# A transformer block on one core: output weights centred on the chip, second norm and residual addition as one VectorE instruction per chunk

## The reference

```python
x = x + LN(attn(LN(x)))     # l1 norm inside, l2 norm outside
x = x + LN(ffn(LN(x)))      # l3 norm inside, z norm outside

def attn(x):
    q = silu(x @ Wq1 @ Wq2)
    f = sigmoid(x @ Wk1 @ Wk2); a = exp(log_sigmoid(f)); k = 1 - a
    h = scan over the tokens of  a * h + k * (x @ Wv)
    out = q * h
    out = out * rsqrt(mean(out * out) + 1e-6) * norm_w      # 512 features
    return out @ Wo                                         # to 256 features

def ffn(x):                 # 6 blocks, a layer norm with gain and bias between them
    x = gelu(x @ W1.T + b1) @ W2.T + b2 + x                 # 256 -> 1024 -> 256
```

## Time and profile before

| | us |
|---|---|
| median of 3 runs (663.36 to 664.93) | 663.96 |
| the profiled execution's own time | 664.71 |
| its span, first to last instruction | 662.9 |
| PE busy | 641.2 (97%) |
| DVE busy | 450.7 (68%) |
| ACT busy | 411.6 (62%) |
| POOL busy | 282.6 (43%) |

### The profile page before, as it was taken

The page is one execution under the profiler, slowest core; times in us unless marked ns, Lnnn a source line. Parts: engine busy times, 40 slices in busy tenths (PEclk is TensorE's granted clock), DMA queues, the critical chain, the costliest instruction groups (busy, mean ns, idle before and its releaser), DMA issues.

```text
span 662.9 us, 8828 instructions
## 1 busy us (share of the span) xinstructions
PE 641.2 (97%) x3017; PEld 533.7 (81%) x3017; DVE 450.7 (68%) x743; ACT 411.6 (62%) x682; POOL 282.6 (43%) x253
## 2 busy tenths in 40 slices
PE   5987999999999999999999999999999999999996
PEld 4766888888888888888888888888888888888886
DVE  3779665687766877668766776776588657665535
ACT  4889696786856655557555566555575555564433
POOL 4997452478624632227422266123282321222203
PEclk8999799999999999999999999999999999999999
DMA  7121000001200300002100003000020000000001
GB/s 279 64 65 33 1 0 1 1 0 34 96 0 1 127 1 1 0 1 84 44 2 0 1 32 96 1 0 1 0 64 1 0 1 0 1 1 32 33 2 64
DMA packets 8685, 19.36 MB, mean 29 GB/s; under 512 B 1600, under 2 KB 4672, under 8 KB 8640
## 3 DMA queue, kind: packets, MB, share of 16 engines
q1 hardware_dynamic: 8064, 18.27, 8.3%
q10 hardware_dynamic: 576, 0.52, 0.2%
HBM read 16.69 MB, written 2.10 MB: 28 GB/s over the span
## 4 chain that ended last, share of the span: by engine, by line
PE 89%; POOL 0%; DVE 0%; POOLq 0%; issue 0%; DVEq 0%
PE BK L417 44%; PE BK L686 38%; PE BK L510 2%; PE BK L696 2%; PE BK L556 1%; PE BK L391 1%; PE BK L736 0%; PE BK L573 0%; PE BK L523 0%; PE BK L610 0%; POOL RS L635 0%; POOLq L173 0%; DVE R L643 0%; DVE ST L629 0%; POOL VE L632 0%
## 5 line engine op out<-in xcount | busy, mean ns | idle before, releaser
L672 ACT ACTIVATE HH<-BK,B 128x512 fp32r<-128x512 f32 x192 | 132.5, 690 | 204.6 <-PE BK L417 204.3
L678 DVE TENSOR_TENSOR HL<-BK,HH 128x512 fp32r<-128x512 f32 x192 | 130.9, 684 | 81.2 <-ACT BK L675 80.8
L417 PE MATMUL BK<-XH,WL 128*128 128x512 f32 x432 | 171.6, 397 | 1.4 <-DVE XL L404 1.4
L417 PE MATMUL BK<-XH,WH 128*128 128x512 f32 x432 | 169.5, 392 | 0.0
L417 PE MATMUL BK<-XL,WH 128*128 128x512 f32 x432 | 169.2, 392 | 0.0
L686 PE MATMUL BK<-HH,WL 128*128 128x512 f32 x368 | 146.7, 399 | 0.0
L686 PE MATMUL BK<-HL,WH 128*128 128x512 f32 x368 | 143.6, 390 | 0.0
L686 PE MATMUL BK<-HH,WH 128*128 128x512 f32 x368 | 143.2, 389 | 0.0
L675 ACT ACTIVATE BK<-BK,B 128x512 f32<-128x512 f32 x192 | 125.7, 655 | 0.0
L417 PEld LDWEIGHTS BK<-XH,WL 128*128 128x128 f32 x432 | 81.9, 190 | 18.3 <-DVE XL L404 1.8
L417 PEld LDWEIGHTS BK<-XH,WH 128*128 128x128 f32 x432 | 81.7, 189 | 18.1
(11 more groups left out here) (106 smaller groups left out, 803.8 us busy)
## 6 DMA issues: line engine op xcount, KB each, us to landing
STG<-in_w SPq DMA_DIRECT2D x24, 512.0 KB, 3.6
out<-R SPq DMA_DIRECT2D x16, 128.0 KB, 1.9
X<-in_x SPq DMA_DIRECT2D x3, 512.0 KB, 8.1
R<-in_wv SPq DMA_DIRECT2D x1, 512.0 KB, 6.3
STG<-in_wo SPq DMA_DIRECT2D x1, 512.0 KB, 7.1
X<-in_x ACTq DMA_DIRECT2D x2, 128.0 KB, 3.1
X<-in_x SPq DMA_DIRECT2D x2, 128.0 KB, 2.8
R<-in_wq SPq DMA_DIRECT2D x1, 256.0 KB, 5.2
```

Source lines behind the costliest of these rows:

```text
L417: r = e.matmul(dst, s, m, start=first and i == 0, stop=last and i == len(todo) - 1)
L672: lambda e, ev=ev, hs=hs, bias=bias: e.activation(HH[:, hs, :], bank_of[ev][:, :], ACT.Gelu, bias=bias),
L678: lambda e, ev=ev, hs=hs: e.tensor_tensor(HL[:, hs, :], bank_of[ev][:, :], HH[:, hs, :].bitcast(f32), ALU.subtract), ("hlo", n, j))
```

## The change

The mean over the 256 features of (out @ Wo) is out @ (row mean of Wo). With each row of Wo centred, the product has mean zero, so the l2 norm is a multiplication by `RS` alone, and `X + product * RS` is one `scalar_tensor_tensor` on VectorE that reads PSUM. The centring is done on VectorE: one sum over [128, 4, 256], one tiny scaling by -1/256, and four `tensor_scalar` that add the negative mean and multiply by norm_w; the last four replace GpSimd's `wo_scaled`. The four `l2_nm` on ScalarE, the four `x1` and two small instructions on GpSimd go away in each tile. The keys of the l3 norm are 1 to 2 lower. `proj(t + 1, 0)` and the first `mm2` of n = 2 now wait for the four `x1`. The ring's banks 2 and 3 are no longer given to `mm1` of the last step. `LASTS` has new entries for the new operations.

```diff
--- before.py
+++ after.py
@@ -32,7 +32,7 @@
 LASTS = {"sync": 0.1, "scalar": 0.6, "vector": 0.68, "gpsimd": 1.31, "tensor": 1.36,
          "_st": 0.41, "_mv": 0.15, "_nm": 0.42, "_rs": 1.03, "_ve": 0.2, "_ng": 0.2, "_nb": 0.2, "ms": 0.15,
          "turn": 0.88, "zk": 0.69, "zq": 0.69, "rms": 0.45, "proj": 1.44, "t2": 0.72, "scan": 1.31, "olo": 0.85,
-         "x1": 0.86, "spin": 6.0, "idle_in": 0.5, "inj": 1.8, "end": 0.72, "wp_hi": 1.06, "wp_lo": 1.31, "wv_lo": 2.5, "wo_lo": 2.5, "wo_scaled": 1.94, "bias": 0.2, "nw": 0.2,
+         "x1": 0.47, "wo_sum": 1.1, "wo_mean": 0.1, "spin": 6.0, "idle_in": 0.5, "inj": 1.8, "end": 0.72, "wp_hi": 1.06, "wp_lo": 1.31, "wv_lo": 2.5, "wo_lo": 2.5, "wo_scaled": 0.36, "bias": 0.2, "nw": 0.2,
          "ghi": 0.69, "gf": 0.65, "ctr": 0.84, "xlo": 0.8, "sum1": 1.41, "sum2": 1.41, "mu": 0.15, "va": 0.15,
          "vae": 0.15, "rsd": 3.0, "ft": 0.25, "fin0": 0.4, "fin1": 0.83}
 HOP = 0.21
@@ -54,7 +54,10 @@
 
     def kept(who):
 
-        return shut | set(range(RING, RING + EARLY)) if who[0] == "mm1" else shut
+        if who[0] != "mm1":
+            return shut
+        last = who[1] == 4 * NB - 1
+        return shut | set(range(RING - 2 if last else RING, RING + EARLY))
 
     def lasts(e, done):
         if done is None:
@@ -217,6 +220,7 @@
         RS = sb("RS", [128, NT, 4])
         MS = sb("MS", [128, NT, 4])
         NM = sb("NM", [128, NT, 4])
+        WM = sb("WM", [128, 4])
         NBS = sb("NBS", [128, NT, 4])
         HALF = sb("HALF", [128, 1])
         BK = [ctx.enter_context(nc.psum_tensor(f"BK{i}", [128, TOK], f32)) for i in range(8)]
@@ -298,12 +302,16 @@
             a = AW[w]
             split(key, raw[w], WH[:, 1, a:a + size[w]], WL[:, 1, a:a + size[w]], "w" + w,
                   [("ldw_" + w,)], lo_waits=[("l1_nm", 0, c) for c in range(4)], lo_engine="vector" if w in ("q1", "k1") else "gpsimd")
-        op("gpsimd", -2, [("ldw_o",), ("nw",)],
-           lambda e: e.tensor_tensor(STG[:, 0, :].rearrange("p (m n) -> p m n", m=4),
-                                     STG[:, 0, :].rearrange("p (m n) -> p m n", m=4),
-                                     NW[:, :].unsqueeze(2).to_broadcast([128, 4, 256]), ALU.mult),
-           ("wo_scaled",))
-        split(0.5, raw["o"], WH[:, 1, 2560:3584], WL[:, 1, 2560:3584], "wo", [("wo_scaled",)])
+        op("vector", -3, [("ldw_o",), ("after", ("ulo", 0, 1))],
+           lambda e: e.tensor_reduce(WM[:, :], STG[:, 0, :].rearrange("p (m n) -> p m n", m=4),
+                                     mybir.AxisListType.X, ALU.add), ("wo_sum",))
+        op("vector", -2.9, [("wo_sum",)],
+           lambda e: e.tensor_scalar(WM[:, :], WM[:, :], -1 / 256, 1.0, ALU.mult, ALU.mult), ("wo_mean",))
+        for m in range(4):
+            op("vector", -2.8 + 0.1 * m, [("wo_mean",), ("nw",)],
+               lambda e, m=m: e.tensor_scalar(STG[:, 0, 256 * m:256 * m + 256], STG[:, 0, 256 * m:256 * m + 256],
+                                              WM[:, m:m + 1], NW[:, m:m + 1], ALU.add, ALU.mult), ("wo_scaled", m))
+        split(0.5, raw["o"], WH[:, 1, 2560:3584], WL[:, 1, 2560:3584], "wo", [("wo_scaled", m) for m in range(4)])
 
         def piece(p):
 
@@ -366,13 +374,15 @@
                 op("gpsimd", key + gap * 4 + 0.5, every,
                    lambda e: e.tensor_scalar(VE[:, t, :], MV[:, t, :, 1], EPS_LN, 1.0, ALU.add, ALU.mult),
                    (name + "_ve", t))
-            op("gpsimd", key + gap * 4 + 0.55, every,
-               lambda e: e.tensor_scalar(NM[:, t, :], MV[:, t, :, 0], -1.0, 1.0, ALU.mult, ALU.mult), (name + "_ng", t))
+            if name != "l2":
+                op("gpsimd", key + gap * 4 + 0.55, every,
+                   lambda e: e.tensor_scalar(NM[:, t, :], MV[:, t, :, 0], -1.0, 1.0, ALU.mult, ALU.mult), (name + "_ng", t))
             op("gpsimd", key + gap * 4 + 0.6, [(name + "_ve", t), ("mhalf",)],
                lambda e: e.tensor_tensor(RS[:, t, :], VE[:, t, :], MH[:, 0:4], ALU.pow),
                (name + "_rs", t))
-            op("gpsimd", key + gap * 4 + 0.7, [(name + "_rs", t), (name + "_ng", t)],
-               lambda e: e.tensor_tensor(NBS[:, t, :], NM[:, t, :], RS[:, t, :], ALU.mult), (name + "_nb", t))
+            if name != "l2":
+                op("gpsimd", key + gap * 4 + 0.7, [(name + "_rs", t), (name + "_ng", t)],
+                   lambda e: e.tensor_tensor(NBS[:, t, :], NM[:, t, :], RS[:, t, :], ALU.mult), (name + "_nb", t))
 
         def norm(key, name, t, dst, src, gap=0.0, extra=()):
             for c in range(4):
@@ -511,7 +521,7 @@
                                          stop=(m == 3 and i == 2), skip_group_check=True)
                     return r
                 op("tensor", M + 8.8, [("olo", t, m), ("ohi", t, m), ("wo_lo",)]
-                   + ([("after", ("proj", t, m - 1))] if m else [("l2_nm", t - 1, c) for c in range(4)] if t else []), proj, ("proj", t, m))
+                   + ([("after", ("proj", t, m - 1))] if m else [("x1", t - 1, c) for c in range(4)] if t else []), proj, ("proj", t, m))
 
             for m in range(1, 4):
                 op("gpsimd", A + 2.0 + (LONG - 2) / 4 * m + 8.6,
@@ -531,14 +541,13 @@
                lambda e, t=t: e.tensor_scalar(MS[:, t, :], bank_of["rms", t][:, 0:4], EPS_LN / 512, 16 * EPS_RMS * EPS_LN,
                                               ALU.mult, ALU.add), ("ms", t))
             stats(Z + 1, "l2", t, p_of, lambda c, t=t: [("proj", t, m) for m in range(4)], 0.4)
-            norm(Z + 4.5, "l2", t, R[:, t], p_of, 0.3, [("turn", "l1", t, k) for k in range(2)])
             for c in range(4):
-                op("gpsimd", Z + 5.5 + 0.6 * c, [("l2_nm", t, c)],
-                   lambda e, t=t, c=c: e.tensor_tensor(X[:, t, c, :], X[:, t, c, :], R[:, t, c, :], ALU.add),
-                   ("x1", t, c))
-            stats(Z + 7, "l3", t, x_of, lambda c, t=t: [("x1", t, c)], 0.4)
-            norm(Z + 11.5, "l3", t, R[:, t], x_of, 0.3, [("x1", t, c) for c in range(4)])
-            turn(Z + 13, "l3", t, [("l3_nm", t, c) for c in range(4)], ("mm1", t, 7))
+                op("vector", Z + 4.5 + 0.4 * c, [("l2_rs", t), *x_in(c)],
+                   lambda e, t=t, c=c: e.scalar_tensor_tensor(X[:, t, c, :], p_of(c), RS[:, t, c:c + 1], X[:, t, c, :],
+                                                              ALU.mult, ALU.add), ("x1", t, c))
+            stats(Z + 6, "l3", t, x_of, lambda c, t=t: [("x1", t, c)], 0.4)
+            norm(Z + 9.5, "l3", t, R[:, t], x_of, 0.3, [("turn", "l1", t, k) for k in range(2)])
+            turn(Z + 11, "l3", t, [("l3_nm", t, c) for c in range(4)], ("mm1", t, 7))
         def layer_norm(E, n, b, t):
 
             p, name = n % 2, f"f{b}"
@@ -699,7 +708,7 @@
                 free = [("after", ("mm2", n, j - 1))]
                 if j == 0:
                     free = ([("claim", RING + i) for i in range(EARLY)] if n == 0 else
-                            [("l2_nm", NT - 1, c) for c in range(4)] if n == 2 else
+                            [("x1", NT - 1, c) for c in range(4)] if n == 2 else
                             [("y", max(n - 2, n // 2), k) for k in range(2)] if n < 4 * NB - 2 else
                             [("z_nm", n - 2, c) for c in range(4)])
                 if n == 4 * NB - 1:
```

## The result

The changed kernel took 669.43 us, median of four runs (668.97 to 670.12), against 663.66 (663.25 to 664.93) for the kernel before beside it. The ratio is 1.0083, 95% interval 1.0071 to 1.0095: 5.8 us slower. The forecast was 659.3, the range ended at 665.5, and slower had 0.14. All of it was missed.

A forecast was written before the change was run, and what follows sets the result against it. PE, busy 97% of the span, bounds the kernel, so only its idle time counts. Gains of 4.0 (tile 0) and 0.7 (output weights) sum to 4.7 us: 660.0 from the profiled 664.71, 659.3 as median; range 654.5 to 665.5.

The forecast's parts named there:

- tile 0's l3 norm now comes some 6 us sooner: Tile 0, without ACT's queue and POOL's 4.18 us: its transposes, then FFN products, can fill PE; part of taking 4.0 us.
- with the same steps from there to PE `proj(1, 2)` starts at 65.3: PE's longest wait, before 67.20: scan done at 62.2, `o` at 62.3 in place of 64.23, gain 1.9 us.
- those FFN products can fill PE there: Around the products `u` of tile 2: earlier FFN work fills PE, so 4.0 us taken between 2.9 and 4.8.
- The 2.9 us of clock: PE from 67 to 73 us: the half-speed stretch after the 3.08 us wait would be gone, 2.9 us.
- `x1` 0.40 each, 1.6 us, bounds 1.4 and 1.9: Tile 0's four new additions on DVE: 1.6 us, not hidden, ahead of the scan of (1, 2).
- Output weights: Wo's centring moved onto DVE at some 21 us, 3.0 us of work: gain 0.7 us before `proj(0, 0)`, bounds +1.5 and -2.5.
- third rival: Wo's chain holds up the first quarter: wait before `proj(0, 0)` 4.1 us, 667.5 us; chance 0.14.
- the first `o` after 29.3 us: POOL's first `o`, which ran at 29.26 before: a later start was listed as a sign that the forecast is wrong.
- second rival: DVE takes POOL's place: `x1` and l3 statistics ahead of scan and `OL`, wait near 3 us, 664.0 us; chance 0.14.
- tiles 1 to 3 free: Norms of tiles 1 to 3: nothing gained, PE busy all through, provided DVE's extra 1.6 us per tile never delays PE.
- the banks kept from `mm1` free: Ring banks 2 and 3 at the last step: taken as nothing, up to 1 us of wait if held longer.
- a slowdown of 0.35 us: DVE's scan beside POOL's additions took 1.57 us against 1.22: 0.35 us would come back, counted in the 0.8.

The follow-up runs named there:

- norm_only: Changed kernel with Wo scaled on GpSimd as before and no centring: 664.44 us, ratio 1.0009 to the kernel before.
- The single moves: Changed kernel, lists kept, one POOL sum of squares moved: (1, 1) behind tile 0's small l3 instructions, 666.21 us; (0, 3) ahead of tile 3's small l1 instructions, 666.45.
- the other HOPs: Changed kernel replanned with another assumed engine-to-engine time in place of 0.21: 0.25 gave 665.96 us, 0.23 gave 666.34.
- x1_short: Changed kernel with both POOL sums of squares moved and tile 0's new additions on 16 of 256 columns: 665.19 us, ratio 1.0022 to the kernel before.
- wo_only: Kernel before with Wo centred on VectorE and the new bank rule, old l2 norm and addition: 663.32 us, ratio 0.9994.
- old_tile0: Changed kernel with the old l2 norm and addition (ACT, POOL) for tile 0 alone: 664.37 us, ratio 1.0003 to the kernel before.
- wo_short: Changed kernel with both POOL sums of squares moved, Wo's sum and scaling on 16 of 256 columns: 665.36 us, ratio 1.0026 to the kernel before.
- two_moves: Changed kernel, lists kept, POOL's sums of squares (1, 1) and (0, 3) both moved: 666.70 us, ratio 1.0046 to the kernel before.

## Why the prediction was wrong, step by step

- **The step that failed: "tile 0's l3 norm now comes some 6 us sooner", and with it "with the same steps from there to PE `proj(1, 2)` starts at 65.3".** These terms took the lists of before and shifted entries in them. In the changed kernel ScalarE's four l3 norms began at 69.92; in the kernel before at 70.00, not 6 us later:

```profile
70.00 2.06 ACT L380 ACTIVATE R<-X,NBS,RS 128x256 f32<-128x256 f32 x4
```

The planner had put these norms' transposes and the first `u` of tile 2 ahead of `proj(1, 2)`, which ran at 75.96. Its scan, forecast to end at 62.2, ended at 67.58 behind the additions and statistics on DVE, and its `o` waited on POOL until 69.84. *norm_only* shows that the 5 us can come: its norms began at 64.86. With both halves they were eaten: PE was 2.6 us late at tile 0's rms product, and the sum of squares of (1, 1) held `VE` for another 2.5 us. The single moves price the two places of POOL's sums at 3.2 and 3.0 us, the other HOPs price the order as a whole at 3.1 to 3.5. The place of `proj(1, 2)` alone is priced by no run, and *norm_only* has it at no cost. The text knew that "a changed operation can also change the order of others" and priced it at nothing ("those FFN products can fill PE there").
- **The 2.9 us of clock** was wrong in size and in kind. The half-speed stretch did not go: 0.50 from 72 to 75, and a second one from 55 to 58. The premise, that only the wait of 3.08 us was followed by half speed and the shorter ones were not, did not hold either: the longest wait just ahead of the second stretch was 0.91 us, at 53.43. And the clock is not worth its share. Of 19 runs of the kernel before beside the first four experiments, four have a mean granted clock of 0.985 and took 664.0 us on average, seven with 0.987 to 0.989 took 664.3, eight with 0.991 or more took 663.5. A clock lower by 0.006 would be 4 us of 664 if all work were PE's; the difference is 0.5. The changed kernel's four runs say the same: the one with 0.991 took 669.04, the others, with 0.984 or 0.985, 668.97 to 670.12. A likely reason, not tested: where other engines feed PE, slow work fills time in which it would have waited.
- **"`x1` 0.40 each, 1.6 us, bounds 1.4 and 1.9"**: the four took 1.63. The price was right. That they stand on the path was right too, but with the wrong sign: *x1_short* points to 1 to 1.5 us of loss through `proj(1, 0)`, which waits for all four. The forecast said "nothing" there, since `x1` would end sooner than `l2_nm` did. It ended at 62.51 (60.88 + 1.63), where the last `l2_nm` had ended at 60.12. These 2.4 us are not the additions' own, though: tile 0's rms product was 2.6 us late already, and in *norm_only*, where it was on time, `proj(1, 0)` started at 60.31, before at 60.26.
- **Output weights, "I take 0.7, bounds +1.5 and -2.5"**: DVE's part took 1.21 + 1.25 + 1.37 = 3.8 us, outside the bounds of 2.2 to 3.7, because the tiny instruction took 1.25 in place of 0.16. The first `o` starts at 31.13, 1.9 us late, inside the lower bound. Not all of that is Wo's: with the same lists up to there it starts at 29.79 in *wo_only* and at 31.73 in *old_tile0*, so the first 20 us differ by up to 1.9 us between executions. Its worth at the end is a loss of about 1.3 us (*wo_short*), and none when it is alone (*wo_only*). Named as the sign of the third rival ("the first `o` after 29.3 us"), it was seen.
- **The third rival ended near the result (667.5 against 669.4) by another way.** That its number is near is luck. Its mechanism, the first quarter held up, is the smaller part; the wait before `proj(0, 0)` was 1.71 us against 1.63, not the 4.1 of that rival.
- **The second rival** named a mechanism that did come: `x1` and the l3 statistics went ahead of `OL` and the scan on DVE, a wait of PE stayed near 3 us (3.46) and the clock fell. It had 0.14 and 664.0 us. That queue stands the same way in *norm_only* and costs nothing there. The second queue, on POOL, the engine that was relieved, no rival had.
- **Right**: the waits for `OL` shrank (7.6 to 2.0 us), though in part because transposes now stand in front of `proj(1, 2)` and wait in its stead; tiles 1 to 3 free (*old_tile0*); the banks kept from `mm1` free (the lists are the same); the end untouched.

The sum, as far as the runs carry it: about 3 us for the order found, some 1.5 us for tile 0's `x1` and some 1.3 us for Wo, both on DVE, make 5.8. The last two are likely and not shown: only under the orders of *two_moves* were they measured, and since the moves of entries did not add up, these need not either. Of why the two halves, each free alone, cost this together, *norm_only* shows a part: the same places in the lists are harmless while the inputs come early enough. The rest stays open.

## What to carry to other kernels

Where a planner or a fixed list sets each engine's order, a change of operations is two changes. Plan both versions with a few values of a constant that means nothing, and time them, before a difference of 1% is put down to the operations. Here another constant alone moved the time by up to 4.6 us, and the edit under its better orders by about 2. An engine that is mostly idle can still be the bound through one entry of its list that waits for something late while ready work stands behind it; look in its timeline for a long wait followed by instructions without a bracket, and take as its price not the wait but the time for which the input of the next entry had been ready (2.5 us here, 0.3 us in *norm_only* behind a wait of 2.62).

## What the runs showed of the hardware

**DVE and POOL shut each other out for a whole instruction.** The scan of 28.18 started while POOL's `WL` ran (27.56 + 2.41 = 29.97). An undisturbed scan keeps DVE for 1.1 us from its start to the next instruction (1.13 from 59.75 to 60.88). 29.97 + 1.1 is 31.07, and the scan ended at 31.05. The one of 65.29 met the sum of squares (65.18 + 1.32 = 66.50), and 66.50 + 1.1 is its end, 67.58. Cut in four, POOL's instruction let the scan in after its first piece (1.20 us) and itself lost the 1.3 us. The Trainium skill, SBUF — State Buffer, section Who interferes with whom, calls the shared ports an exclusive lock and counts a VectorE instruction with two SBUF inputs, as the scan is, among those that contend with GpSimd's reads. That whoever issues first holds them for the whole instruction and the other blocks fully, it says of VectorE's two-port modes; the rows show the same for the scan. The prediction had used the same section for a slowdown of 0.35 us, and missed that against one POOL instruction of 2.4 us the price is up to 1.7.

**A tiny instruction can be caught as well.** The `tensor_scalar` of 128x4 with SBUF in and out (L309) took 1.25 us; the one of the same size that reads PSUM takes 0.16. It started at 23.18, POOL's two `WL` (L348, 21.84 and 2.56 us long) ended at 24.40, the tiny one at 24.43. In *wo_short* it started at 22.86, just before the first of the two `WL` gave way to the second, and took 0.27. There the four multiplications on 16 columns were caught in its place: they began at 23.64, while POOL's second `WL` ran until 24.37 (21.81 + 2.56), and took 1.35 us. The same section says that `tensor_scalar` may run in a mode that takes the shared ports. The sum (L306, 1.21 us for 1024 elements) began before POOL did and shows nothing of it.

**A long wait of PE isn't always followed by half clock.** 3.08 us before 67.20 were followed by 0.50 until 73, 3.46 us before 72.25 by 0.50 until 75, and in *norm_only* 2.96 us before 67.20 by 1.00. And half clock isn't always preceded by a long one: the stretch of 55 to 58 in the changed kernel came after a wait of 0.91 us.
